# Softmax denominators taken per key tile in 128 columns, and four smaller moves, in a Flamingo block on one core

## The reference

```python
def reference(x, ctx_1024, g_xattn, g_ffn, w_gate, w_up, w_down):
    # attention without a mask; rotary positions on q and k, a linear bias per head
    q = layernorm(x); k = v = ctx_1024
    scores = einsum('bqhd,bkhd->bhqk', rope(q), rope(k)) * scale + bias
    attn = softmax(scores, axis=-1)
    x = x + tanh(g_xattn[0]) * einsum('bhqk,bkhd->bqhd', attn, v)
    ...
    x = x + tanh(g_ffn[0]) * quantised_ffn(layernorm(x), w_gate, w_up, w_down)
    return x
```

## Time and profile before

| what | value |
|---|---|
| median of 3 runs | 1749.58 us (1749.09 to 1751.61) |
| the profiled execution | 1751.76 us, its span 1749.9 us |
| PE busy | 1602.6 us, 92% |
| DVE busy | 1449.6 us, 83% |
| ACT busy | 1221.1 us, 70% |
| POOL busy | 838.9 us, 48% |
| first maxima on PE | 28.0 us from the span's start |
| last exponential of the attention | about 907 us |

### The profile page before, as it was taken

The page is one execution under the profiler, slowest core; times in us unless marked ns, Lnnn a source line. Parts: engine busy times, 40 slices in busy tenths (PEclk is TensorE's granted clock), DMA queues, the critical chain, the costliest instruction groups (busy, mean ns, idle before and its releaser), DMA issues. The chain is left out here.

```text
span 1749.9 us, 37267 instructions
## 1 busy us (share of the span) xinstructions
PE 1602.6 (92%) x14821; PEld 637.6 (36%) x14821; DVE 1449.6 (83%) x2082; ACT 1221.1 (70%) x1941; POOL 838.9 (48%) x504
## 2 busy tenths in 40 slices
PE   3899999999999999999979999999999950899999
PEld 0233333333333333333325444444444420344444
DVE  7899999999999888888857998868989989755451
ACT  3688888888889888988753332329997987754450
POOL 5699899999999999998740010100000000000000
PEclk9999999999999999999999999999999975899999
DMA  6678889888799787877577898649998999986661
GB/s 156 154 149 174 169 173 182 158 170 173 152 176 182 149 175 160 171 156 140 115 175 189 266 261 271 219 153 324 347 348 275 335 354 387 287 277 216 217 217 60
DMA packets 377182, 367.94 MB, mean 210 GB/s; under 512 B 217872, under 2 KB 288912, under 8 KB 369072
## 3 DMA queue, kind: packets, MB, share of 16 engines
q1 hardware_dynamic: 368080, 300.55, 61.8%
q0 software_dynamic: 8928, 65.02, 19.0%
HBM read 154.08 MB, written 95.42 MB: 143 GB/s over the span
## 5 line engine op out<-in xcount | busy, mean ns | idle before, releaser
L1463 DVE TENSOR_REDUCE cm<-quad 128x1 f16<-128x1024 f32 x512 | 600.2, 1214 | 64.8 <-PE quad L1005 63.9
L1244 ACT ACTIVATE P<-quad 128x512 f32<-128x512 f32 x1024 | 556.8, 598 | 114.0 <-PE quad L1018 102.2
L2072 POOL TENSOR_TENSOR Ps<-P,P 128x2048 f32<-128x2048 f32 x93 | 440.6, 4738 | 45.2 <-ACT P L1244 45.2
L1018 PE MATMUL quad<-QA,KA 101*32 101x512 f16 x4096 | 366.1, 385 | 6.8 <-ACT P L1244 5.3
L1005 PE MATMUL quad<-KA,QA 100*32 100x512 f16 x4096 | 334.3, 391 | 35.6 <-DMA QA<-S 18.1
L1069 PE MATMUL quad<-P,cg 128*32 128x512 f32 x2048 | 265.5, 594 | 0.0
L1097 PE MATMUL quad<-x_hl,Wg 128*128 128x512 f16 (+1 forms) x1200 | 249.1, 370 | 1.3 <-DVE x_hl L1759 1.0
L1097 PE MATMUL quad<-x_hl,Wu 128*128 128x512 f16 x1152 | 248.8, 379 | 0.0
L1158 PE MATMUL quad<-Wd,oh 128*128 128x512 f16 x768 | 228.6, 379 | 0.0
L1018 PEld LDWEIGHTS quad<-QA,KA 101*32 101x32 f16 x4096 | 105.1, 94 | 299.3 <-ACT P L1244 231.1
L1325 ACT ACTIVATE ev<-quad 128x1024 f32<-128x1024 f32 x95 | 96.2, 1013 | 109.3 <-PE quad L1097 103.3
(11 more groups left out here) (169 smaller groups left out, 1938.3 us busy)
## 6 DMA issues: line engine op xcount, KB each, us to landing
Ps<-P POOLq DMA_DIRECT2D x62, 1024.0 KB, 8.1
gate_scratch<-ev SPq DMA_DIRECT2D x48, 512.0 KB, 3.8
gt<-gate_scratch SPq DMA_DIRECT2D x48, 512.0 KB, 5.6
up_scratch<-ev SPq DMA_DIRECT2D x48, 512.0 KB, 4.3
ud<-up_scratch SPq DMA_DIRECT2D x96, 256.0 KB, 3.6
x_words<-up_scratch SPq DMA_DIRECT2D x45, 512.0 KB, 11.4
gated_scratch<-gq SPq DMA_DIRECT2D x48, 256.0 KB, 4.1
gd<-gated_scratch SPq DMA_DIRECT2D x96, 128.0 KB, 4.3
```

Source lines behind the costliest of these rows:

```text
L1018: mm = e.matmul(K.score[h % 2][j:j + 32, :], K.KA[p % 2][0:101, kt, h, j:j + 32], K.QA[p % 2][0:101, 4 * qc:4 * qc + 4, h, :], start=True, ...
L1244: e.activation(K.Pb[pb][:, h, :], K.score[h % 2], ACT.Exp, scale=SCALE / (QPOW * KPOW)).then_inc(K.a_exp, 1)
L1463: e.tensor_reduce(cm[:, col:col + 1], K.quad[UNIT["max", hm, u] % 2][:, :], AX.X, ALU.max).then_inc(K.v_max, 1)
L2072: e.tensor_tensor(K.Ps[n][:, :, :], K.Pb[(st.g - 1) % NP][:, :, :], K.Pb[st.g % NP][:, :, :], ALU.add).then_inc(K.g_sum, 1)
```

## The change

What it does, part by part:

- **Denominators per tile.** POOL's sum of tiles 6 and 7 is gone. PE takes tiles 6 and 7 straight from their `P` buffers, in steps 0 and 1 of the next half, `Ps0` in step 6 and `Ps2` in step 2: four jobs for a half in place of three. The exponential that reuses such a buffer now waits for PE's job.
- **128 columns.** `pick` (four matrices of 128 by 32 with ones in column `qt`) takes the place of `ones`. Each job is 16 matmuls over 128 queries in place of 4 over 512; the result is 128 by 128. ACT's copy has 128 columns, and one transpose turns it.
- **Statistics of the second norm** move from steps 6, 7 and 0 to steps 0, 1 and 2. The aggregation in three places moves two steps along.
- **Maxima.** One transpose instruction over 128 partitions in place of four, then four small DMAs in place of one.
- **Start.** After two operations on POOL, DVE does the rest of the first deviations in five.

```diff
-        self.sum = (hf, s // 2) if last and s % 2 == 1 else (hf, {1: 0, 4: 2, 7: 1}[s]) if inside and s % 3 == 1 else None
+        self.sum = (hf, s // 2) if last and s % 2 == 1 else (hf, {1: 0, 4: 2}[s]) if inside and s in (1, 4) else None
-        if s == 6 and inside:
-            self.dens = (hf, 0)
-        elif s in (1, 2) and 1 <= hf < NHALF:
-            self.dens = (hf - 1, s)
+        if s in {0: 6, 1: 7, 2: 2} and 1 <= hf < NHALF:
+            self.dens.append((hf - 1, {0: 6, 1: 7, 2: 2}[s]))
+        if s in {6: 0} and inside:
+            self.dens.append((hf, {6: 0}[s]))
...
-        elif w == 0 and 1 <= p < NQ:
-            self.stats = (p - 1, 0, 2)
+        elif w in (0, 1, 2) and 1 <= p < NQ:
+            self.stats = (p - 1, 0, (0, 1, 2).index(w))
...
-        e.wait_ge(K.v_row, 4 * hf + 4)
-        row = K.QA[p % 2][100:101, 4 * qc:4 * qc + 4, :, :].rearrange("o i h q -> o (i h) q")
-        e.dma_start(row, K.crow[k][0:16, :]).then_inc(K.d_crow[k], 16)
+        e.wait_ge(K.v_row, hf + 1)
+        for i in range(4):
+            row = K.QA[p % 2][100:101, 4 * qc:4 * qc + 4, :, 32 * i:32 * i + 32].rearrange("o i h q -> o (i h) q")
+            e.dma_start(row, K.crow[k][32 * i:32 * i + 16, :]).then_inc(K.d_crow[k], 16)
...
+        elif n > 5:
+            src = K.Pb[(8 * hf + n) % NP]
+            e.wait_ge(K.a_exp, score_no(hf, n, 3))
...
-            mm = e.matmul(K.den[32 * h:32 * h + 32, :], K.ones[:, :], K.Ps[n % 2 if hf == NHALF - 1 else n][:, h, :], start=n == 0, stop=n == (3 if hf == NHALF - 1 else 2))
+            for qt in range(4):
+                for h in heads:
+                    mm = e.matmul(K.den[32 * h:32 * h + 32, :], K.pick[:, qt, :], src[:, h, 128 * qt:128 * qt + 128],
+                                  start=n == first and qt == 0, stop=n == final and qt == 3)
...
-        for i in range(4):
-            e.transpose(K.crow[hm % 2][:, 32 * i:32 * i + 32], K.cm[hm % 2][32 * i:32 * i + 32, :]).then_inc(K.v_row, 1)
+        e.transpose(K.crow[hm % 2][:, :], K.cm[hm % 2][:, :]).then_inc(K.v_row, 1)
...
+    def first_deviations():
+        mean, rs, nm = K.mv1[:, 0:4, 0], K.rs1[:, 0:4], K.nm1[:, 0:4]
+        shifted, guess, square, factor = [t[:, 0:4] for t in K.nwt]
+        e.wait_ge(K.g_r1, 2)
+        e.tensor_tensor(square, guess, guess, ALU.mult).then_inc(K.v_first, 1)
...
```

More of the change, by code:

```diff
@@ L212, in all_steps @@
             if st.p < NQ:
-                steps[i + 1].aggregate = st.p // 4 - 1
+                steps[i + 3].aggregate = st.p // 4 - 1
     for b, p in enumerate(DEVIATION_GROUPS):
@@ L267, in den_no @@
 def den_no(hf, n):
-    return 3 * hf + n + 1
+    return 4 * hf + (n if hf == NHALF - 1 else DEN_ORDER.index(n)) + 1
 def sum_no(hf, n):
-    return 3 * hf + (1, 3, 2)[n]
+    return 2 * hf + n // 2 + 1
 def rope_no(p, w):
@@ L402, in __init__ @@
         self.cm = [A(f"cm{i}", [128, 32], F16) for i in range(2)]
-        self.crow = [A(f"crow{i}", [32, 128], F16) for i in range(2)]
+        self.crow = [A(f"crow{i}", [128, 32], F16) for i in range(2)]
         self.st1 = [A(f"st1{i}", [128, 6], F32) for i in range(2)]
@@ L1029, in denominators @@
     def denominators(hf, n):
-        if n == 0 and hf > 0:
+        last = hf == NHALF - 1
+        first, final = (0, 3) if last else (DEN_ORDER[0], DEN_ORDER[-1])
+        if n == first and hf > 0:
             e.wait_ge(K.a_den, hf)
-        if hf == NHALF - 1:
+        if last:
+            src = K.Ps[n % 2]
             e.wait_ge(K.v_sum, n + 1)
-        else:
[L1035 to L1040, removed]
+        elif n > 5:
+            src = K.Pb[(8 * hf + n) % NP]
+            e.wait_ge(K.a_exp, score_no(hf, n, 3))
+        else:
+            src = K.Ps[n]
+            e.wait_ge(K.d_acc[n // 2], 16 * hf + 16)
+        halves = ((0, 1), (2, 3)) if last and n == 3 else ((0, 1, 2, 3),)
+        for heads in halves:
+            if heads == (2, 3):
                 e.wait_ge(K.v_sum, 5)
-            mm = e.matmul(K.den[32 * h:32 * h + 32, :], K.ones[:, :], K.Ps[n % 2 if hf == NHALF - 1 else n][:, h, :], start=n == 0, stop=n == (3 if hf == NHALF - 1 else 2))
+            for qt in range(4):
+                for h in heads:
+                    mm = e.matmul(K.den[32 * h:32 * h + 32, :], K.pick[:, qt, :], src[:, h, 128 * qt:128 * qt + 128],
+                                  start=n == first and qt == 0, stop=n == final and qt == 3)
         mm.then_inc(K.pe_den, 1)
@@ L1059, in tensor_program @@
             score(st.hf, st.s, 3)
-        if st.s == 1 and st.dens is not None:
-            denominators(*st.dens)
+        if st.s in (1,):
+            for job in st.dens:
+                denominators(*job)
         if before is not None and before.inside:
@@ L1073, in tensor_program @@
             hf = st.out
[L1074 to L1077, removed]
-                for i in range(4):
[L1079 to L1082, removed]
+            e.wait_ge(*K.bank_release(("out", hf), 0))
+            e.wait_ge(K.a_den, hf + 1)
+            e.transpose(K.bank(("out", hf), 0)[:, 0:128], K.denT[:, :], ident).then_inc(K.pe_tden, 1)
+            e.wait_ge(*K.bank_release(("out", hf), 1))
+            e.wait_ge(K.a_num, hf + 1)
+            for i in range(4):
+                mm = e.transpose(K.bank(("out", hf), 1)[:, 128 * i:128 * i + 128], K.numT[:, 128 * i:128 * i + 128], ident)
+            mm.then_inc(K.pe_tnum, 1)
+        if st.s not in (1,):
+            for job in st.dens:
+                denominators(*job)
         before = st
@@ L1961, in deviation, with first_guesses @@
         step_of(rs, nw[1], nw[3], ALU.mult, sem, base + 7)
+    def first_guesses():
+        e.wait_ge(K.g_half, 6)
+        e.wait_ge(K.v_mv1, 4)
+        step_of(K.nwt[0][:, 0:4], K.mv1[:, 0:4, 1], K.eps[:, 0:4], ALU.add, K.g_r1, 1)
+        step_of(K.nwt[1][:, 0:4], K.nwt[0][:, 0:4], K.half[:, 0:4], ALU.pow, K.g_r1, 2)
     def deviation_1(first, last, base):
```

102 lines of the change are left out of this document (57 added, 45 removed).

## The result

The changed kernel takes **1873.89 us** (median of 4 runs, 1866.56 to 1878.88) against 1749.95 (4 runs, 1749.09 to 1751.61): ratio 1.0704, interval 1.0673 to 1.0735. It is 124 us slower where I forecast 21 us faster, and outside the range.

A forecast was written before the change was run, and what follows sets the result against it. PE and DVE were taken to bound the attention alternately, step by step. From the profiled 1751.8 us, 19.9 (27.3 less 7.4) and 1.1 for the start gave 1730.8; as that run was 2.2 above the median, 1729, range 1712 to 1775.

The forecast's parts named there:

- DMAs: Row of maxima from step 5: issues and landing take 3.9 us, first waiting score 6.2 us on, so hidden by 2.3.
- Short jobs: A denominator job on PE in short matmuls over 128 columns takes 0.87 us, against 0.86 for the long form.
- The rival with 57 ns a pair: PE issues short matmuls slower than their columns: a job takes 1.84 us, kernel 1850, or 1790 half hidden; chance 0.20.
- The step table: Attention half, summed step by step over whichever engine sets each: 25.78 us, 0.91 under the mean of 26.69.
- What comes off: Collisions in step 2 of odd and first halves, and ACT in late even halves, take 7.4 of 27.3 us gain.
- the 1.5 for the first three halves: Step 2 of the first three halves, with a statistic of x there, loses 1.5 us of the gain in all.
- the 7.4: Total us deducted from the 27.3 us gain over halves 1 to 30 for collisions and ACT, leaving 19.9.
- Step 5: Transposes of maxima on DVE go from 0.90 to about 0.2 us, so PE sets this step at 2.66.
- Start: Before the attention: first deviations moved to DVE take 1.1 us off the first maxima, at 28.04 before; bounds 0 to 3.8.
- The eaten room: Rival: steps 5 to 7 stay near 2.84 us while step 0 pays 0.66; half 26.3, kernel 1745; chance 0.13.
- halves that do not get shorter: Rival: PE's wait for POOL was no cost, step 1 stays 4.1 us; kernel 1743, within the 1740 to 1750 band.
- POOL: Removing the sum PE waited for, 0.46 us in step 1, also gives POOL 4.7 us of room in 26.7.

The follow-up runs named there:

- rows_two_queues: Changed kernel with the last two of its four row DMAs issued from ACT's queue behind the next step's second exponential; 1760.99 us, ratio 1.0062 to the kernel before.
- one_row: Changed kernel with the maxima's four transposes and the single row DMA put back; 1753.31 us, ratio 1.0021 to the kernel before.
- columns_alone: Kernel before with only the denominators put into 128 columns (three jobs of 16 matmuls, one transpose, shorter copy on ACT); 1745.93 us, ratio 0.9979.
- one_row_late: The one_row kernel with its single row DMA issued some 2 us later, after POOL's accumulating DMA; 1888.74 us, ratio 1.0803 to the kernel before.
- sum_after_rows: Changed kernel with POOL's accumulating DMA of step 6 held until the four row DMAs have landed; runs of 1777.27, 1778.14, 1815.54 and 1879.26 us.

## Why the prediction was wrong

**The step that failed** is the one headed DMAs: "Four issues of 528 ns and a landing of 1.8 us make 3.9 us ... Hidden by 2.3 us, with SP's queue free at that place". The issues took 2.44 us, 0.3 more than four times 528, which the cover would have borne. The landing of 1.8 us did not hold, and the cover was worth nothing with it: it is the landing of a DMA that goes out ahead of POOL's accumulating DMA. The timeline of the kernel before had the two side by side:

```profile
397.04 0.53 SPq L722 DMA_DIRECT2D QA<-crow  x1
397.33 0.85 POOL L2051 DMA_DIRECT2D Ps<-P  x1
```

The cover that counted was 0.3 us from issue to issue, and not 2.3 us of landing; of four in a row the last is out 1.3 us after POOL began, and lands up to 8.4 us after its issue. I had looked at SP's queue and at none of the others, though the accumulating DMA of the same step stood in the code and in the trace. I named the sign of it ("scores of step 0 waiting for the rows from `crow`") and the price, "each us past it would cost up to 31 us", but gave the case no chance. That price was also too low by the clock: a mean wait of 3.5 us in 23 halves is 80 us, and the runs show 121. That 121 is already less what the single transpose gives.

**Point by point for the rest.** *Short jobs*, 0.87, "the one value on which the sign hangs": right. In the changed kernel the group behind a job of 32 starts 0.87 us after it:

```profile
952.25 1.05 PE L1052 MATMUL quad<-P,pick 128*32 128x128 f32 x32
953.12 1.03 PE L1081 MATMUL quad<-P,cg 128*32 128x512 f32 x8
```

That is 27 ns a pair of weight load and matmul. The rival with 57 ns a pair (1790 to 1850 us) is out. So is, for this kernel, the floor of some 62 ns for each matmul that the Trainium skill (TensorE: Matmul & The Clock Gate, the section on the gap of 56 ns) gives where instructions are decoded in software; 27 ns agrees with the other floor there, about 25 ns between starts. The changed kernel did come out near the 1867 us of that estimate, by another mechanism altogether.

*The step table*: right to 0.03 us in the sum for half 1 (25.81 against 25.78), which is luck in part: step 2 is 0.17 over the forecast, steps 1 and 5 are 0.11 and 0.12 under it. In the even halves step 1 has 3.81 even without a collision, against 3.65. *What comes off* was right where I looked and short elsewhere: in rows_two_queues the odd halves 5, 7, 9, 11 and 13 have 4.06 in step 2, as forecast 0.5 to 0.6 above 3.52. Half 3 (4.26 against 3.69 before) I count to the 1.5 for the first three halves. But halves 15 and 16 are longer too (4.93 and 5.24 against 4.34 and 4.64), and so is step 3 of halves 9 and 17 (4.23 and 4.24 against 3.08 and 3.09) and of half 25 (3.43 against 2.84). That is 0.6 x 3 + 1.15 x 2 = 4.1 us that the 7.4 lacked. *Step 5*: right, 2.65 against 2.66 with the single transpose (rows_two_queues); but none of the kernels that ran has it for nothing. The run one_row has 26.77 in the mean, 0.99 over the 25.78. Step 5 is 0.58 over the forecast, step 7 0.21 over and step 6 0.31 under, which I put down to the transposes in four parts; steps 1 and 2 are 0.19 and 0.18 over the forecast, steps 3 and 4 0.08, step 0 0.06. So without the stall my 1729 would have been missed as well: one_row less the 0.48 x 31 = 15 us of its transposes is about 1738, and rows_two_queues less the 22 us of ACT's issues 1739. Both are estimates; no run shows that time.

*Start*, -1.1: PE's first maxima stand at 27.23 against 28.04, -0.8. But the place moves from trace to trace: with the old start it lies between 27.81 and 28.70 in five traces (mean 28.29), with the new one between 26.89 and 27.44 in five (mean 27.15). That is -1.1, as forecast. *The eaten room* and *halves that do not get shorter*: small beside the stall, and without it one_row, at 1753, is above both their bands. *POOL*: its wait is gone, but it was worth 0.21 us a half in step 1 and not the 0.46 of half 12, since one half had stood for all.

**What stays open.** Not measured: 128 columns with tiles 6 and 7 direct and the statistics left where they were, and the same, or the changed kernel as it is, with three row DMAs on SP's queue and only the fourth on ACT's. By the parts measured alone the first would be at 1749.9 + 3.9 - 4.0 less 1.1 for the start, 1749. If, with tiles 6 and 7 direct, step 1 does not take back the 0.14 us a half that it took in columns_alone, it is some 4 us less. The best that ran is 128 columns alone, 4 us under the kernel before. Some stalls within a job are also open: in one_row PE issues 21 of 32 short matmuls of a job at 408.18 and the other ones only from 409.88 on, with no releaser that the profile shows,

```profile
409.88 0.52 PE L1051 MATMUL quad<-P,pick 128*32 128x128 f32 x10 [0.87 <-issue]
```

while SP's DMA transpose is in flight. That instructions reached PE late is a guess that no experiment here tested. The short form does not seem to bring it: the weight loads of the jobs have 55 us of such idle time before them in one_row, 50 in columns_alone, and 48.5 in the kernel before.

## What to carry to other kernels

A landing time belongs to a place among all queues, not to a DMA: before splitting or delaying a small transfer that PE waits for, look up what large DMA any other queue issues in the next microseconds, and count from the last of the split issues. Here one small DMA, issued some 1.8 us behind the large one in place of 0.4 us ahead of it or more, cost 8% of the kernel. Take the price of a removed wait from the mean over all loops, odd and even, never from the one that is at hand; and price a new stall of PE of several us above its length, for the clock: the one looked at here cost 1.6 times its length, and the kernels with 80 to 88 us of such waits came out 106 to 135 us longer, 1.2 to 1.5 times.

## What the runs showed of the hardware

- A row DMA of 4 KB lands after 1.7 us in the median when it goes out ahead of the 1024 KB accumulating DMA, and after 6.3 us when mostly behind it (one_row, one_row_late). In the changed kernel the 64-byte packets of a late one stand between packets of 8192 bytes.
- A wait of PE of 4.58 us brought the granted clock to 1.2 GHz, and the 6.02 us behind it had 0.54. In the changed kernel 23 waits of 3.5 us went with at most 53 us of lost full-speed work.
- Matmuls over 128 columns with 32-wide column tiles, each with its own weight load, run at 27 ns a pair (32 pairs in 0.87 us).
- In one place a DMA transpose and the accumulating DMA in flight together landed after 28.1 and 20.6 us (sum_after_rows, started at 104.66 and 104.80); in five others of that run the sum took 7.5 to 9.1 us beside one. What made the difference is open.
- Issuing two row DMAs from ACT's queue took 1.16 us of ACT's time in the place shown, and cost some 0.7 us of the half by the estimate above (rows_two_queues).
